# Ten of fifty dense subchunks of a graph attention's products moved from one stage to the next

## The chip, the cores and the metric

One core of one Trainium2 chip runs the whole program in one launch. The metric is the device time of that core in microseconds (us). A profile is one execution of the same program, taken by the hardware profiler.

## The reference

The program computes four residual graph layers over 100,000 nodes of 16 features and 50,000 edges sorted by destination: x = x + layer(relu(layernorm(x)), edges). The change is in the first, an attention network with two attention layers. What it computes, cut to the part that matters:

```python
def _gat_layer(x, src, dst, W, a_s, a_d, b, heads, outc):
    h = (x @ W).reshape(N, heads, outc)
    alpha_s = (h * a_s).sum(-1)
    alpha_d = (h * a_d).sum(-1)
    e = leaky_relu(alpha_s[src] + alpha_d[dst], SLOPE)
    m = segment_max(e, dst)
    p = exp(e - m[dst])
    z = segment_sum(p, dst)
    alpha = p / (z[dst] + 1e-16)
    out = segment_sum(h[src] * alpha[:, :, None], dst)
    return out.reshape(N, heads * outc) + b
# src, dst: the edges and a loop at each node
h = selu(_gat_layer(x, src, dst, W1, a_src1, a_dst1, b1, 3, 32))
h = selu(_gat_layer(h, src, dst, W2, a_src2, a_dst2, b2, 1, 32))
return h @ Wf + bf
```

A node without an incoming edge has only its own loop, so its attention is 1 and the first layer gives x @ W1 + b1 there: "dense" work that needs no edges. The others are done by "slots", one for each edge in order of destination, where the last slot of a destination holds the node's sum.

## The kernel before

The program is a row of stages, each a block in which every engine has its own list of instructions; behind each stage all engines meet at a barrier, and its semaphores are cleared. Engines wait for each other through counting semaphores (`hold`, `wait_ge`).

**Stage A** (lines 465 to 773, tiles a_...) makes three things side by side.
- DVE and PE count the edges by destination (28 groups of one-hot products for each half of the table: lines 547, 548, 652), and then DVE works out where each node's row goes.
- The dense half: 10 chunks (k) of 80 columns, each of 5 subchunks (n) of 16 columns, for all 128 partitions. SP loads a chunk of x (line 754). DVE makes its layer norm in seven pieces spread between other work (`norm_part`, lines 593 to 613, 448, 449). For a subchunk, PE transposes it (`flip`, 665), ACT copies the result to a_norm_t (715), PE makes the scores (`score`, 673), which ACT copies to a row (724), and in four quarters u: PE makes the first layer's products (`up`, 682), ACT the two activations of selu (739, 741), DVE joins them (634), PE multiplies by the second layer's weights (700), and DVE adds the constant (`send`, 624). SP stores the rows of x and scores of a chunk to t_gat1 (765) and those of the second layer of each subchunk to t_gat2 (770).
- POOL gathers the rows of x for the edges: 392 indirect DMAs (line 530), of 128 rows each. The first 112 follow the counting; the later 280 are paced by the dense half, six for the four activations of a subchunk (`joins`, a wait on act_ok). Before each batch of eight it waits until the batch before has landed.

Then comes the sorting stage (lines 778 to 960), and one that loads the sorted slots and begins to gather from t_gat1.

**Stage B** (lines 1150 to 1463, tiles g_...) is the first layer's attention over 400 slot columns. POOL gathers 336 columns of neighbours' rows (line 1208), at most about two entries ahead of DVE. DVE goes through "entries" of 48 columns (the last three of 32, 16 and 8): `edge_score` (1332 to 1345) when the entry's gathers have landed, `edge_sum` (1358 to 1372: 51 scans), `edge_mix` (1411 to 1423). Each entry feeds three chunks of 16 columns (25 in all). For a chunk: PE transposes (`flip`, 1231), ACT copies to g_mix_t (1285), PE makes four quarters of products (1245, three banks of PSUM in turn, so that the fourth waits for the first's activations), ACT two activations (1313, 1315), DVE joins (1460), PE the second products (1256), all four after one another, and DVE the rows (`send`, 1433, 1435). DVE's order by chunk: send of the chunk before, four joins, then the edge work due: the score of the next entry at the entry's second chunk, its sum and mix at the third. ACT's order: eight activations, the edge work's exponentials, and only then the copy of the next chunk.

DVE's order before, whole:

```python
for n in range(NCH):
    if n:
        send(n - 1)
    for u in range(4):
        hold(dve, exp_ok, 4 * n + u + 1)
        v.scalar_tensor_tensor(act_t[:, u], ex[:, u], 1.0, pos[:, u], ALU.min, ALU.add
                               ).then_inc(act_ok, 1)
    edges(n)
send(NCH - 1)
```

Behind stage B stands the second layer's attention, which gathers from t_gat2.

## Time and profile before

| | us |
|---|---|
| median of 3 runs | 6252.12 |
| lowest, highest | 6250.92, 6256.97 |
| the profiled execution | 6259.5 |
| its span, first to last instruction | 6257.5 |
| PE busy | 2760.5 (44%) |
| DVE busy | 3563.7 (57%) |
| ACT busy | 1272.2 (20%) |
| POOL busy | 4345.7 (69%) |
| stage A, first gather to the next stage's first DMA | 64.5 to 778.7 |
| stage B, to the next stage's first DMA | 1457.6 to 2046.4 |

PE is TensorE, DVE VectorE, ACT ScalarE, POOL GpSimd, SP the engine that only issues DMAs. Busy times overlap between engines, and none says what a stage waits for. A row of a timeline has the start in us from the span's start, the duration, the engine, the line of the kernel, the operation, and in brackets how long the engine stood idle before it and what ended that. A row of busy times by stretch has the stretch and its length, then busy us (and instructions) of PE, PEld (the weight loads), DVE, ACT and POOL, then the granted TensorE clock as a share of full speed, the DMA share and GB/s.

### The profile page before, as it was taken

To read this page: it belongs to the slowest core of one execution; us is meant where nothing else is said; L and a number is where in the kernel's file an instruction comes from. 1 tells how busy PE (TensorE), PEld (TensorE's weight loads), DVE (VectorE), ACT (ScalarE), POOL (GpSimd) and SP (SyncE) were. 2 spreads that over 40 slices of the span, in tenths; PEclk is the share of its full clock that TensorE was granted. 3 is DMA by queue.
4 is the path that set the end of the run, shared out by engine and by line. 5 is a ranking of instruction groups with operands and counts; after the bars stand their busy time and mean duration, and the time that the engine had idled before them with its cause. 6 is when DMAs were issued, how large, how long until landed. Compare 5 with 4: busy or idle time off the path is not lost. (4 is left out here: it accounts for less than half of the span.)

```text
span 6257.5 us, 46239 instructions
## 1 busy us (share of the span) xinstructions
PE 2760.5 (44%) x13424; PEld 2086.1 (33%) x13424; DVE 3563.7 (57%) x8977; ACT 1272.2 (20%) x2042; POOL 4345.7 (69%) x3949
## 2 busy tenths in 40 slices
PE   5789677753544455346655542111111035553000
PEld 2477533333434344345544432111111013432000
DVE  8855399977556666673447777433322138886000
ACT  0166377741322233211111110000000011000000
POOL 4766566667773677477767776888888844777776
PEclk9899899985665555566667675555555567776555
DMA  2022133321110422123322222222222235221001
GB/s 44 10 72 63 51 80 78 77 74 12 20 20 16 99 70 64 46 72 101 101 83 67 65 70 79 44 38 38 41 29 26 8 97 174 60 57 33 7 7 47
DMA packets 283361, 350.20 MB, mean 56 GB/s; under 512 B 133518, under 2 KB 204432, under 8 KB 281970
## 3 DMA queue, kind: packets, MB, share of 16 engines
q1 hardware_dynamic: 112158, 295.24, 14.1%
q0 software_dynamic: 169376, 41.40, 8.9%
q10 hardware_dynamic: 1576, 10.60, 0.7%
q8 instruction: 109, 1.79, 0.1%
q14 instruction: 142, 1.16, 0.1%
HBM read 231.06 MB, written 122.29 MB: 56 GB/s over the span
## 5 line engine op out<-in xcount | busy, mean ns | idle before, releaser
L2412 POOL DMA_INDIRECT acc<-l_rows,l_uniq x392 | 625.1, 1595 | 121.5 <-issue 108.6
L530 POOL DMA_INDIRECT pay<-in_x,gidx x392 | 462.4, 1180 | 239.9 <-DMA pay<-in_x,gidx 116.1
L2453 PE MATMUL ps_l<-l_msg,l_alike 128*128 128x16 f32 x784 | 176.3, 375 | 960.1 <-DVE l_msg L2516 960.1
L1547 POOL DMA_INDIRECT g_ring<-t_gat,idx x392 | 423.9, 1081 | 230.5 <-issue 112.3
L2682 POOL DMA_INDIRECT l_ring<-t_last,idx x392 | 385.1, 982 | 268.1 <-ACTq L2676 148.1
L1877 POOL DMA_INDIRECT r_ring<-t_rel,idx x392 | 427.5, 1091 | 186.4 <-issue 109.1
L2398 POOL DMA_INDIRECT l_ring<-t_mix,idx x392 | 422.4, 1078 | 155.0 <-issue 119.1
L836 POOL DMA_INDIRECT t_sort<-pay,c_pos x392 | 381.6, 973 | 207.0 <-DVE c_pos L920 103.8
L2188 POOL DMA_INDIRECT r_ring<-t_rel,idx x392 | 399.6, 1019 | 152.2 <-issue 110.7
L2453 PEld LDWEIGHTS ps_l<-l_msg,l_alike 128*128 128x128 f32 x784 | 171.0, 331 | 965.4 <-DVE l_msg L2516 965.4
L2692 POOL DMA_INDIRECT fin<-X,home_i x393 | 376.9, 959 | 119.8 <-issue 119.8
L1208 POOL DMA_INDIRECT ring<-t_gat,src_i x336 | 377.7, 1124 | 109.9 <-issue 91.4
L2723 PE MATMUL ps_l<-w_rel,l_pick 128*128 128x256 f32 x784 | 258.2, 501 | 246.1 <-DVE l_pick L2752 246.1
L2511 DVE TENSOR_SCALAR l_den<-l_ring 128x128 f32<-128x128 f32 x49 | 11.2, 229 | 560.0 <-DMA l_ring<-t_mix,idx 560.0
L2723 PEld LDWEIGHTS ps_l<-w_rel,l_pick 128*128 128x128 f32 x784 | 199.3, 261 | 304.7 <-DVE l_pick L2752 265.0
L955 PE MATMUL ps_c<-coarse,c_hit 128*128 128x400 f16 x784 | 262.1, 334 | 3.9 <-ACT c_hit L855 3.9
L955 PE MATMUL ps_c<-fine,c_hit 128*128 128x400 f16 x784 | 262.1, 334 | 0.0
L2465 ACT COPY l_rows<-ps_l 128x128 f32<-128x128 f32 x49 | 13.0, 265 | 1139.7 <-PE ps_l L2453 1139.7
L700 PE MATMUL ps_a<-w_ext,a_act_t 96*128 96x128 f32 x1600 | 224.1, 285 | 39.7 <-DVE a_row L624 39.2
L700 PEld LDWEIGHTS ps_a<-w_ext,a_act_t 96*128 96x128 f32 x1600 | 214.9, 200 | 60.4 <-DVE a_row L624 49.1
L915 DVE SCALAR_TENSOR_TENSOR c_junk<-iota_lo,lo_f,ps_c 128x400 f32<-128x400 f16 x392 | 230.9, 625 | 5.5 <-PE ps_c L955 5.5
L634 DVE SCALAR_TENSOR_TENSOR a_act_t<-a_ex,a_pos 96x512 f32<-96x512 f32 x200 | 137.3, 686 | 143.5 <-ACT a_ex L741 140.0
(540 smaller groups left out, 8470.6 us busy)
## 6 DMA issues: line engine op xcount, KB each, us to landing
c_rows_d<-row_dst SPq DMA_DIRECT2D x98, 256.0 KB
l_keys<-row_at SPq DMA_DIRECT2D x49, 512.0 KB, 4.1
l_typs<-row_typ SPq DMA_DIRECT2D x49, 512.0 KB, 3.7
g_hs<-t_gat SPq DMA_DIRECT2D x30, 660.0 KB, 4.8
acc<-r_zero SPq DMA_DIRECT2D x60, 320.0 KB
t_rel<-r_row SPq DMA_DIRECT2D x30, 640.0 KB, 3.6
r_hs<-t_rel SPq DMA_DIRECT2D x30, 640.0 KB, 4.7
d_gain<-acc SPq DMA_DIRECT2D x30, 640.0 KB
```

The costliest lines, as they stand in the source:

```text
L530: pool.indirect_dma_start(pay[:, s, 8:PAY], None, x, bass.IndirectOffsetOnAxis(gidx[:, s:s + 1], 0)).then_inc(gat_in[s // BATCH], 16)
L700: last = mm(ps[:, at:at + WIDE], act_t[:, u, P * m:P * (m + 1)], w2_ext[:], start=True, stop=True, skip_group_check=True)
L836: pool.indirect_dma_start(t_sort, bass.IndirectOffsetOnAxis(pos[:, e:e + 1], 0), pay[:, e, :], None).then_inc(sent, 16)
L955: last = mm(ps[:, bank:bank + LO], hit[:, q % 2, j, col:col + P], part[:, LO * j:LO * (j + 1)], start=(j == 0 and m == 0), stop=(j == 1 an ...
L1208: pool.indirect_dma_start(ring1[:, s, :], None, t_gat1, bass.IndirectOffsetOnAxis(src_i[:, s:s + 1], 0)).then_inc(gat_in[s // BATCH], 16)
L1547: pool.indirect_dma_start(ring[:, s % (NR * QN), :], None, t_gat2, bass.IndirectOffsetOnAxis(idx2[:, s:s + 1], 0)).then_inc(gat_in[s // BA ...
L1877: pool.indirect_dma_start(ring[:, s % (NR * QN), :], None, table, bass.IndirectOffsetOnAxis(idx2[:, s:s + 1], 0)).then_inc(gat_in[s // BAT ...
L2188: pool.indirect_dma_start(ring[:, s % (NR * QN), :], None, t_rel2, bass.IndirectOffsetOnAxis(idx2[:, s:s + 1], 0)).then_inc(gat_in[s // BA ...
L2398: pool.indirect_dma_start(ring[:, s, :], None, t_mix, bass.IndirectOffsetOnAxis(idx2[:, s:s + 1], 0)).then_inc(gat_in[s // BATCH], 16)
L2412: pool.indirect_dma_start(acc[r], bass.IndirectOffsetOnAxis(uniq[:, s:s + 1], 0), rows[:, (s // ES) % RR, s % ES, :], None, compute_op=ALU.add
L2682: pool.indirect_dma_start(ring[:, s, :], None, t_last, bass.IndirectOffsetOnAxis(idx2[:, s:s + 1], 0)).then_inc(gat_in[s // BATCH], 16)
L2723: last = mm(ps[:, at:at + 256], pick[:, e % 2, s], w_rel[:].rearrange("p i o -> p (i o)"), start=True, stop=True)
```

## The change

Every fifth dense subchunk (the last of each chunk) keeps its layer norm, transpose, copy and scores in stage A, but its products are not made there. Its transposed, normalised columns go to a tile of their own and to a new table in DRAM, t_late, of 128 x 256 numbers for each of ten. Stage B loads them two jobs ahead and works through a list of 35 jobs: dense 0 and 1, then the 25 slot chunks, with a dense job behind each odd one up to the fifteenth. POOL's pacing in stage A becomes seven gathers for four activations. In stage B the order within a job changes too: the products of the next job stand between those of this one, ACT copies the next chunk (into the other of two tiles) after the first quarter, and DVE's send comes after the first join. The diff, without renamed counters:

```diff
+    heavy = [n for n in range(NSUB) if n % PER != PER - 1]
+    NH = len(heavy)
+    assert T - 2 * NB <= 7 * NH and PER == 5 and SUB * FEAT == t_late.shape[2] and ND == t_late.shape[1]
...
+    late_s = [sem("late0"), sem("late1")]
+
+    def flat_of(n):
+        if n % PER == PER - 1:
+            return late[:, (n // PER) % 2]
+        return norm_t[:, heavy.index(n) % 3]
+
...
-        part, turn_no = divmod(s - 2 * NB, 6)
-        joins = 4 * part + (0, 1, 1, 2, 3, 3)[turn_no]
+        part, turn_no = divmod(s - 2 * NB, 7)
+        joins = 4 * part + turn_no // 2
         if part < 0 and s % 2 == 0 and s >= 4:
             hold(pool, hist_ok, s // 2 - 1)
-        elif joins > 0 and turn_no not in (2, 5):
+        elif joins > 0 and turn_no % 2 == 0:
             hold(pool, act_ok, joins)
         if s >= BATCH and s % BATCH == 0:
...
-        for n in range(NSUB):
+        for i, n in enumerate(heavy):
             if n + 2 < NSUB:
                 flip(n + 2)
             for u in range(4):
-                if n and u % 2 == 0:
-                    hold(pe, row2_ok, 2 * (n - 1) + u // 2 + 1)
-                hold(pe, act_ok, 4 * n + u + 1)
+                if u == 2 and n % PER == PER - 2:
+                    if n + 3 < NSUB:
+                        flip(n + 3)
+                    score(n + 1)
+                if i and u % 2 == 0:
+                    hold(pe, row2_ok, 2 * (i - 1) + u // 2 + 1)
+                hold(pe, act_ok, 4 * i + u + 1)
...
-                if n + 1 < NSUB:
-                    up(n + 1, u)
-            if n + 1 < NSUB:
-                score(n + 1)
+                if i + 1 < NH:
+                    up(i + 1, u)
+            if i + 1 < NH:
+                score(heavy[i + 1])
...
+            if n % PER == PER - 1:
+                if n // PER >= 2:
+                    hold(act, score_ok, n - 2 * PER + 1)
+                    act.wait_ge(late_s[(n // PER) % 2], 16 * (n // PER // 2))
+            elif heavy.index(n) >= 3:
+                hold(act, score_ok, heavy[heavy.index(n) - 3] + 1)
+            nc.scalar.copy(flat_of(n), ps[:, FLIP:FLIP + SUB * FEAT]).then_inc(copy_ok, 1)
...
+                if u == 3 and n % PER == PER - 2:
+                    if n + 3 < NSUB:
+                        turn(n + 3)
+                    take_scores(n + 1)
...
-            if n % PER == PER - 1:
-                hold(sp, scored, n + 1)
+            if n % PER == PER - 2:
+                hold(sp, scored, n + 2)
                 hold(sp, row_ok, k + 1)
                 sp.dma_start(t_gat1.rearrange("(p c) f -> p c f", c=C)[:, k * Q:(k + 1) * Q, :], row[:, k % 2]
                              ).then_inc(out_s[k % 2], 16)
                 if k + 2 < ND:
                     load(k + 2)
-            hold(sp, row2_ok, 2 * (n + 1))
-            sp.dma_start(columns_of(t_gat2, SLOTS + SUB * n, SUB), row2[:, n % 2]).then_inc(out2_s[n % 2], 16)
+                sp.dma_start(t_late[:, k], late[:, k % 2]).then_inc(late_s[k % 2], 16)
+            hold(sp, row2_ok, 2 * (i + 1))
+            sp.dma_start(columns_of(t_gat2, SLOTS + SUB * n, SUB), row2[:, i % 2]).then_inc(out2_s[i % 2], 16)
...
+    LATE = t_late.shape[1]
+    jobs = [("dense", 0), ("dense", 1)]
+    for n in range(NCH):
+        jobs.append(("slot", n))
+        if n % 2 == 1 and len(jobs) - n - 1 < LATE:
+            jobs.append(("dense", len(jobs) - n - 1))
+    NJ = len(jobs)
+    entering = [("slot", n) for n in enter]
+    job_of = [jobs.index(("slot", n)) for n in range(NCH)]
+    assert NJ == NCH + LATE
...
+    mix_t = tmp("mix_t", [HID, 2, 8 * P])
+    late_t = tmp("late_t", [P, 2, Q * FEAT])
...
+        def load(d):
+            sp.dma_start(late_t[:, d % 2], t_late[:, d]).then_inc(late_in[d % 2], 16)
+
+        load(0)
+        load(1)
+        for t, (kind, k) in enumerate(jobs):
+            at = Q * k if kind == "slot" else SLOTS + 5 * Q * k + 4 * Q
+            hold(sp, row_ok, t + 1)
+            sp.dma_start(columns_of(t_gat2, at, Q), row[:, t % 2]).then_inc(out_s[t % 2], 16)
+            if kind == "dense" and k + 2 < LATE:
+                load(k + 2)
...
+        def up(t, u):
+            kind, k = jobs[t]
+            if u == 0 and kind == "slot":
+                hold(pe, copy_ok, k + 1)
+            if u == 0 and kind == "dense":
+                hold(pe, late_in[k % 2], 16 * (k // 2 + 1))
+            if 4 * t + u >= 3:
+                hold(pe, exp_ok, 4 * t + u - 2)
+            bank = 1024 + 512 * ((4 * t + u) % 3)
+            to = ps[0:HID, bank:bank + 512]
+            for j in range(2):
+                if kind == "slot":
                     at = 512 * (u % 2) + 256 * j
                     last = mm(to[:, 256 * j:256 * (j + 1)], w1_half[:, u // 2].rearrange("p h c -> p (h c)"),
-                              mix_t[:, at:at + 256], start=True, stop=True)
-                last.then_inc(up_ok, 1)
-            if n + 1 < NCH and n + 1 not in enter:
-                flip(n + 1)
-            if n:
-                hold(pe, row_ok, n)
+                              mix_t[:, k % 2, at:at + 256], start=True, stop=True)
+                else:
+                    last = mm(to[:, 256 * j:256 * (j + 1)], w1_dense[:, 2 * u + j], late_t[:, k % 2],
+                              start=True, stop=True)
+            last.then_inc(up_ok, 1)
+
+        def down(t, u):
+            kind, k = jobs[t]
+            if t and u == 0:
+                hold(pe, row_ok, t)
+            hold(pe, act_ok, 4 * t + u + 1)
+            for m in range(4):
+                node = 2 * (4 * (u % 2) + m) + u // 2 if kind == "slot" else 8 * (m % 2) + 2 * u + m // 2
+                last = mm(ps_o[:, node // 8, node % 8], act_t[:, u, P * m:P * (m + 1)],
+                          w2_ext[:, 0:CH + 2],
+                          start=True, stop=True)
+            if u == 3:
+                last.then_inc(down_ok, 1)
+
+        for u in range(3):
+            up(0, u)
+        for t, (kind, n) in enumerate(jobs):
+            if t + 1 < NJ and jobs[t + 1][0] == "slot" and jobs[t + 1][1] not in enter:
+                flip(jobs[t + 1][1])
+            if t == 0:
+                up(0, 3)
             for u in range(4):
-                hold(pe, act_ok, 4 * n + u + 1)
-                for m in range(4):
-                    node = 2 * (4 * (u % 2) + m) + u // 2
-                    last = mm(ps_o[:, node // 8, node % 8], act_t[:, u, P * m:P * (m + 1)],
-                              w2_ext[:, 0:CH + 2],
-                              start=True, stop=True)
-            last.then_inc(down_ok, 1)
+                down(t, u)
+                if t + 1 < NJ and jobs[t + 1] not in entering:
+                    up(t + 1, u)
+            if kind == "dense":
+                if t + 1 < NJ and jobs[t + 1] in entering:
+                    flip(jobs[t + 1][1])
+                    for u in range(4):
+                        up(t + 1, u)
+                continue
...
-            if n + 1 in enter:
-                flip(n + 1)
+            if t + 1 < NJ and jobs[t + 1] in entering:
+                flip(jobs[t + 1][1])
+                for u in range(4):
+                    up(t + 1, u)
...
         def copy(n):
             hold(act, flip_ok, n + 1)
-            nc.scalar.copy(mix_t[:], ps[0:HID, 0:8 * P]).then_inc(copy_ok, 1)
+            if n >= 2:
+                hold(act, up_ok, 4 * (job_of[n - 2] + 1))
+            nc.scalar.copy(mix_t[:, n % 2], ps[0:HID, 0:8 * P]).then_inc(copy_ok, 1)
...
         edges(-1)
-        copy(0)
-        for n in range(NCH):
+        for t, (kind, n) in enumerate(jobs):
             for u in range(4):
-                hold(act, up_ok, 4 * n + u + 1)
-                bank = 1024 + 512 * ((4 * n + u) % 3)
+                hold(act, up_ok, 4 * t + u + 1)
+                bank = 1024 + 512 * ((4 * t + u) % 3)
                 view = ps[0:HID, bank:bank + 512]
                 nc.scalar.activation(pos[:, u], view, ACT.Relu, bias=b1_col[:, 1:2],
                                      scale=1.0 / SELU_ALPHA)
                 nc.scalar.activation(ex[:, u], view, ACT.Exp, bias=b1_col[:, 0:1]).then_inc(exp_ok, 1)
-            edges(n)
-            if n + 1 < NCH:
-                copy(n + 1)
+                if u == 0 and t + 1 < NJ and jobs[t + 1][0] == "slot" and jobs[t + 1] not in entering:
+                    copy(jobs[t + 1][1])
+            if kind == "slot":
+                edges(n)
+            if t + 1 < NJ and jobs[t + 1] in entering:
+                copy(jobs[t + 1][1])
...
-        def send(n):
-            b = n % 2
-            hold(dve, down_ok, n + 1)
-            if n >= 2:
-                hold(dve, out_s[b], 16 * (n // 2))
+        def send(t):
+            (kind, n), b = jobs[t], t % 2
+            hold(dve, down_ok, t + 1)
+            if t >= 2:
+                hold(dve, out_s[b], 16 * (t // 2))
             view = row[:, b].rearrange("p (a n) w -> p a n w", n=8)
-            for to, at in ((as2, CH), (ad2, CH + 1)):
+            for to, at in ((as2, CH), (ad2, CH + 1)) if kind == "slot" else ():
                 v.tensor_tensor(to[:, Q * n:Q * (n + 1)].rearrange("p (a n) w -> p a n w", n=8),
                                 ps_o[:, :, :, at:at + 1], const[:, :, :, at:at + 1], ALU.add)
...
-        for n in range(NCH):
-            if n:
-                send(n - 1)
+        for t, (kind, n) in enumerate(jobs):
             for u in range(4):
-                hold(dve, exp_ok, 4 * n + u + 1)
+                hold(dve, exp_ok, 4 * t + u + 1)
                 v.scalar_tensor_tensor(act_t[:, u], ex[:, u], 1.0, pos[:, u], ALU.min, ALU.add
                                        ).then_inc(act_ok, 1)
-            edges(n)
-        send(NCH - 1)
+                if t and u == 0:
+                    send(t - 1)
+            if kind == "slot":
+                edges(n)
+        send(NJ - 1)
```

## Rows read from the trace of the kernel before

**Rows 1.** Busy time of each engine by stretch: stage A's dense part, its end, stage B.
```profile
280.00:724.00 444.00, 403.09 (x2682) 355.47 (x2680) 246.48 (x380) 277.51 (x522) 283.94 (x250) 0.95 0.23 66
724.00:768.00 44.00, 0.00 (x0) 0.00 (x0) 0.00 (x0) 0.00 (x0) 28.44 (x31) 0.53 0.09 12
1458.00:2046.00 588.00, 276.44 (x1418) 225.25 (x1418) 367.62 (x970) 155.79 (x249) 377.67 (x336) 0.62 0.11 18
```
**Rows 2.** Timeline of stage A's end: first gathers of batches, the last, the next stage.
```profile
684.86 0.94 POOL L530 DMA_INDIRECT pay<-in_x,gidx  x1 [1.59 <-DMA pay<-in_x,gidx]
...
721.94 0.94 POOL L530 DMA_INDIRECT pay<-in_x,gidx  x1 [2.10 <-DMA pay<-in_x,gidx]
...
756.96 0.94 POOL L530 DMA_INDIRECT pay<-in_x,gidx  x1 [1.59 <-DMA pay<-in_x,gidx]
...
765.69 0.94 POOL L530 DMA_INDIRECT pay<-in_x,gidx  x1 [0.31 <-issue]
778.73 0.32 SPq L823 DMA_DIRECT2D c_rows_d<-row_dst  x1
```
**Rows 3.** Waits between 260 and 780 us: us in total, times, longest.
```profile
POOL pay L530 <- DMA pay<-in_x,gidx: 91.1, 31, 7.1
```
**Rows 4.** Waits between 1450 and 2050 us.
```profile
DVE g_act_t L1460 <- ACT g_ex L1315: 142.9, 95, 6.5
...
DVE idx L1332 <- DMA ring<-t_gat,src_i: 33.5, 6, 6.5
```
**Rows 5.** Timeline of stage A: PE's second products, two quarters on end.
```profile
699.96 1.06 PE L700 MATMUL ps_a<-w_ext,a_act_t 96*128 96x128 f32 x8
...
701.72 1.06 PE L700 MATMUL ps_a<-w_ext,a_act_t 96*128 96x128 f32 x8
```
**Rows 6.** Timeline of stage A: a gather beside DVE.
```profile
282.79 2.80 POOL L530 DMA_INDIRECT pay<-in_x,gidx  x1 [0.31 <-issue]
...
283.28 1.48 DVE L595 SCALAR_TENSOR_TENSOR a_ln_cent<-a_ln_small,a_xin 128x1280 f32<-128x1280 f32 x1
...
284.80 0.69 DVE L634 SCALAR_TENSOR_TENSOR a_act_t<-a_ex,a_pos 96x512 f32<-96x512 f32 x1
```
**Rows 7.** Timeline of stage B: one entry, from mix to mix, and cold ups.
```profile
1562.27 5.54 PE L1245 MATMUL ps_g<-g_mix_t,w_half 96*96 96x256 f32 x16 [1.10 <-ACT g_mix_t L1285]
...
1625.09 2.56 DVE L1423 TENSOR_TENSOR g_mix<-g_mix,g_S 128x2304 f32<-128x2304 f32 x1
...
1629.74 1.01 ACT L1285 COPY g_mix_t<-ps_g 96x1024 f32<-96x1024 f32 x1 [12.20 <-PE ps_g L1231]
...
1637.74 1.04 PE L1231 MATMUL ps_g<-ident,g_mix 128*96 128x128 f32 x8
...
1638.61 3.66 PE L1256 MATMUL ps_g<-w_ext,g_act_t 96*128 96x34 f32 x32
...
1642.10 3.67 PE L1245 MATMUL ps_g<-g_mix_t,w_half 96*96 96x256 f32 x16
...
1644.38 0.68 ACT L1313 ACTIVATE g_pos<-ps_g,b_col 96x512 f32<-96x512 f32 x1
...
1645.52 0.69 ACT L1313 ACTIVATE g_pos<-ps_g,b_col 96x512 f32<-96x512 f32 x1
...
1647.96 0.69 DVE L1460 SCALAR_TENSOR_TENSOR g_act_t<-g_ex,g_pos 96x512 f32<-96x512 f32 x1 [0.46 <-ACT g_ex L1315]
1655.13 0.20 DVE L1332 CAST idx<-ring 128x48 int32<-128x48 f32 x1 [6.48 <-DMA ring<-t_gat,src_i]
...
1668.03 2.54 DVE L1358 TENSOR_TENSOR g_S<-ring,ps_g 128x2304 f32<-128x2304 f32 x1
...
1694.02 2.56 DVE L1423 TENSOR_TENSOR g_mix<-g_mix,g_S 128x2304 f32<-128x2304 f32 x1
```
**Rows 8.** Timeline of stage B: the mix of entry 0 and that of entry 6.
```profile
1492.34 2.56 DVE L1423 TENSOR_TENSOR g_mix<-g_mix,g_S 128x2304 f32<-128x2304 f32 x1
...
1899.13 2.56 DVE L1423 TENSOR_TENSOR g_mix<-g_mix,g_S 128x2304 f32<-128x2304 f32 x1
```

More of the change, by code:

```diff
@@ L120, in gnn_kernel @@
     row_typ = scratch("row_typ", (T, P))
+    t_late = scratch("t_late", (P, C // 80, 256))
     w_rel_dram = scratch("w_rel_dram", (RELS * FEAT, FEAT))
@@ L499, in gnn_kernel @@
             row2 = tmp("row2", [P, 2, SUB, GAT2])
+            late = tmp("late", [P, 2, SUB * FEAT])
             t = ln_buffers(ctx, Q, "a", 2)
@@ L642, in _ @@
                     for half in range(2):
-                        send(NSUB - 1, half)
+                        send(NH - 1, half)
                 @block.tensor
@@ L690, in _ @@
                     score(0)
-                    for n in range(NSUB):
+                    for i, n in enumerate(heavy):
                         if n + 2 < NSUB:
```

59 lines of the change are left out of this document (22 added, 37 removed).

## The prediction

> **What bounds the kernel now.** I read the chip's whole span first, then the two stages that the change touches, then inside each the one engine whose waits set its end. The program runs in stages with a barrier behind each, so a stage is worth what its last engine saves. The profiled execution took 6259.5 us (its span is 6257.5), 7.4 us above the median of the runs shown, 6252.1. I make the sum against the profiled one and take off 7.4 at the end.
>
> Stage A (the dense half, lines 465 to 773) has its dense chain from 280 to 724 us, and PE is busy 403 of those 444 us. Then comes the stretch to look at: from 724 to 768 PE, DVE and ACT show zero instructions, and POOL alone runs 31 gathers [rows 1]. The stage ends with POOL: its last gather starts at 765.69, and the next stage's first DMA goes out at 778.73 [rows 2]. What holds POOL is itself: 250 gathers in 444 us are 1.78 us each, 31 in 44 us 1.42 us; its longest wait is for the landing of each batch of eight, 91.1 us in 31 waits [rows 3]. The waits on act_ok that pace it never decide: the last gather asks for activation 186 of 200, and the dense chain had made all 200 by 724.
>
> Stage B (slots of the first attention, lines 1150 to 1463, 1458 to 2046 us): PE is busy 276 of 588 us, ACT 156, DVE 368, POOL 378 [rows 1]. It looks like room for ten jobs. But DVE is a chain here. Per 48 columns (an "entry") it does sum and mix, then three chunks of activations, and in between a score that needs POOL's gathers. DVE waits 142.9 us for ACT's exponentials and only 33.5 us, in six waits, for gathers [rows 4].
>
> **Stage A, part by part.** Removed: up, activation, down and send of ten subchunks. In the steady state one quarter of up and down takes PE 1.76 us (from 699.96 to 701.72 [rows 5]), so 7.0 per subchunk and some 65 to 70 us off the dense chain. Kept for all fifty: flip, copy, score, the ten layer norms, the ten loads and ten stores of t_gat1. Of that gain the stage keeps nothing directly: the chain ended 42 us before POOL did, and now ends about 110 before. The new pacing (7 gathers per subchunk in place of 6) asks for 160 activations of 160 at the end and is met just as early. So all that counts is whether POOL gathers faster with less work beside it. Two rows of price. In the last chunk, where there are activations but no layer norm and no load, three batches go from 684.86 to 721.94: 37.08 us for 24 gathers, 1.545 each. The next three, with nothing beside them, go from 721.94 to 756.96: 35.02, 1.459 each [rows 2]. The difference, 0.086 us, times the 37 gathers that fit into 65 us at 1.78, is 3.2 us. That is my value, because activations are what is removed. Upper bound: the whole difference of 1.78 and 1.42 times 37, 13 us; that would need the layer norms and big transfers to go too, and they stay. On the other side I allow 3 us lost, since the same ten layer norms and transfers are packed into a shorter time and the ten stores of late rows (131 KB each) are new. Stage A: **-3 us** (-13 to +3).
>
> A gather does stretch beside DVE: the one at 282.79 took 2.80 us against 0.94, over a centring and the next activation [rows 6]. The Trainium skill (SBUF — State Buffer, "Who interferes with whom") has it that a tensor_tensor with two SBUF inputs takes only the read side of the port pair shared with GpSimd, and infers that descriptor generation needs the write side. By that the removed activations would give POOL nothing and stage A would gain 0; this trace speaks against the inference, since that gather ends only after two-input operations do.
>
> SP's list has ten fewer stores of t_gat2 and ten new ones of late rows; it only follows row2_ok and scored, and nobody waits for it but the buffers' next turn. ACT waits for late_s before it overwrites a late tile, two chunks (over 70 us) after the store was issued: nothing.
>
> **Stage B, part by part.** Prices [rows 7]: a chunk's ups cost PE 3.67 us, its downs 3.66, at the full clock (0.92 a quarter each), a flip 1.04; behind a long idle the ups take 5.54. Copy 1.00, two activations by ACT 1.15 per quarter, DVE's activation 0.69, its rows 1.0.
>
> An entry before, counted from the end of mix (1627.65): the copy ends 3.1 later (1630.75), the second chunk's last activation 17.9 after that (1648.65), then DVE waits until 1655.13 for gathers (6.5), scores for 2.9, reaches sum 12.9 after the score's start (1668.03), and sum and mix take 28.5 (to 1696.58). Without the wait that is 3.1 + 17.9 + 12.9 + 28.5 = 62.4; with it 68.9. So each middle entry has 6.5 us of cover, and one and a half dense jobs to put there.
>
> After, two things change. The dense jobs come in, and the order is new: ups of the next job lie between downs of this one, and ACT copies the next chunk after the first quarter. That copy waits for a flip which PE has behind the four ups. In the steady state a job followed by a slot chunk repeats: flip 1.04, copy 1.00, exponential of the second quarter 1.15, up 0.92, then three quarters of down and up 5.5, with handoffs 10 us; a job followed by a dense one 7.4.
> - Entries 2, 4, 6 (slot, dense, slot, score, slot, sum, mix): copy 3.1; ups end 5.5 and those of the dense job 12.8 after it; flip 13.9, copy 15.0, next up 17.2, its last 22.8, flip 23.8, copy 24.9, three exponentials and the activation 29.1; score 2.8; four prepared quarters of exponentials behind it 5.9; sum and mix 28.5: 69.4.
> - Entries 3 and 5 (dense, slot, slot, score, dense, slot, sum, mix): the dense job's exponentials were made during sum, so it costs DVE 3.8, but PE's downs stand ahead of the flip, and the copy ends 9.1 after mix; the next two chunks 15.6; score 2.8; dense and slot 14.4; 28.5: 70.4.
> - Entry 1 has two dense jobs ahead of the first chunk: copy 15.1 in place of 3.1, then 15.6 + 2.8 + 14.4 + 28.5: 76.4.
>
> Sum over entries 1 to 6: 76.4 + 3 x 69.4 + 2 x 70.4 = 425.4 us, against 1494.9 to 1901.7 = 406.8 before [rows 8]: +18.6. Behind it the copy's stall costs 3.5 at the chunk before the last scores, the saving and the loss of entry 7 cancel (-4, +3.7): about +22. The six gather waits, 33.5 us, are in that: they are the cover, and it is spent. What is late next is ACT's exponential, hence PE's ups.
>
> Bounds: nothing at all if every job fits (0); and 10 jobs of 7.4 less 33.5 of cover, +40, if the new order gives nothing back. Stage B: **+22 us** (0 to +40). The new load of a dense job's rows (131 KB) is issued two jobs ahead, against landings of a few us: nothing; if it were late, PE would stand. Gathers lengthen by some 4 us over the stage (40 more activations) and are off the path by 8 us.
>
> Sum: 6259.5 - 3 + 22 = 6278.5 profiled, less 7.4: **6271 us**.
>
> **Rivals.**
> - The cover is enough (28%). If PE stays at its full clock and handoffs cost less, entries come under the 68.9 of the gathers; then the stage is paced as before and only its tail grows, +3, less 3 in stage A: 6252. For: 33.5 us of waits and PE idle for over half. Against: PE idles through each sum and mix, which the jobs can't fill, and shows 0.62 as mean granted clock in stage B (0.95 in A) [rows 1], so the flip and ups behind it run at 1.2 GHz. It decides if an entry is 1 us or more shorter than I count.
> - POOL is freed (9%): the whole 13 us in stage A, with the stage B of the rival above giving 2 back: 6252 - 13 - 2 = 6237, faster. For: 0.36 us a gather of contention. Against: the last chunk's batches, above.
> - The new order gives nothing back, or PE works the whole stage at 1.2 GHz (8%): the ups then cost 5.54 in place of 3.67, 1.9 us in each of some fifteen chunks and jobs that stand on the chain, +28 on top of +22, 6299.
> - That the change doesn't do what it says: ten of fifty subchunks do move; the products are the same instructions, so there is no such case.
>
> **How the numbers follow.** 55% for my sum, 28, 9 and 8 for the rivals. About 12.5 us (0.2%) is what a measurement can tell. Slower holds most of the first case and the last: 0.60. Same holds the second and a tenth of the first's lower end: 0.30. Faster 0.10. The range leaves out the third case and the last: 6245 to 6294; the likeliest case's own is 6256 to 6290.
>
> **What would show it.** Right: no PE, DVE or ACT work in the last 100 us of stage A, POOL's last gather within a few us of 765.7; in stage B no waits of the score for gathers, entries of 69 to 71 us, ACT waiting for a flip at the copy. Wrong: a stage A shorter by over 8 us (the contention step), or scores that still wait for gathers with entries of 68.9 (the chain step).

## The result and the profile after

| | before | after |
|---|---|---|
| median, us | 6254.55 (4 runs) | 6326.93 (6319.76 to 6338.86, 4 runs) |
| ratio | | 1.0119, 95% interval 1.0103 to 1.0135 |
| the profiled execution, its span | 6259.5, 6257.5 | 6331.7, 6330.0 |
| first gather of x to the last gather's end | 64.5 to 766.6 | 64.2 to 745.7 |
| stage B, its first gather to the next stage's | 1458.3 to 2047.0 = 588.7 | 1438.3 to 2121.0 = 682.7 |

The kernel became 1.2% slower. The forecast was 6271 us with a range to 6294. Slower was right and the size was wrong: stage A gained 21 us where I had 3, and stage B lost 94 where I had 22. The stages between and behind them took the same time to within 3 us.

The busy times by stretch of the changed kernel (columns as in [rows 1]); the first two stretches answer to stage A's, the third to stage B's:

```profile
280.00:658.00 378.00, 335.15 (x2193) 294.01 (x2191) 211.05 (x319) 232.14 (x441) 247.93 (x219) 0.94 0.25 71
658.00:746.00 88.00, 0.00 (x0) 0.00 (x0) 0.34 (x1) 0.00 (x0) 57.54 (x61) 0.51 0.10 15
1438.00:2121.00 683.00, 436.98 (x1900) 366.06 (x1900) 398.21 (x1020) 201.18 (x329) 346.68 (x336) 0.59 0.12 21
1653.00:1745.00 92.00, 63.15 (x248) 54.07 (x248) 46.78 (x109) 23.09 (x37) 46.08 (x48) 0.54 0.13 23
1820.00:1895.00 75.00, 42.39 (x248) 36.50 (x248) 47.00 (x110) 22.88 (x37) 49.56 (x48) 0.70 0.15 27
```

In stage A the dense chain ends 65 us earlier (at 656), as predicted, and POOL works alone for 88 us (VectorE has one instruction of 0.34 us there). In stage B, PE is busy 437 us in place of 276: 161 us more for ten jobs. A job's ups and downs at full clock are 7.3 us [rows 7], so ten are 73, and the rest is slower instructions. The last two rows are the third and the fifth entry, which have the same 248 PE instructions each: 63 us of PE work and 92 us of time at a granted clock of 0.54, against 42 and 75 at 0.70.

The waits of stage B after:

```profile
ACT g_mix_t L1359 <- PE ps_g L1276: 194.2, 25, 15.8
DVE g_act_t L1534 <- ACT g_ex L1388: 188.1, 97, 11.5
...
DVE as L1509 <- PE ps_g L1307: 39.1, 14, 6.3
DVE g_row L1511 <- PE ps_g L1307: 30.9, 7, 6.3
...
POOL ring L1245 <- DVE g_mix L1499: 73.4, 5, 32.1
```

DVE no longer waits for gathers at all (33.5 us before, [rows 4]). The gathers now wait for the mix, and ACT's copy waits for PE's flip, 25 times (before: 101.0 us in 10 waits). The row of before that the second products' rows answer to:

```profile
DVE as L1433 <- PE ps_g L1256: 18.4, 8, 2.4
```

DVE is the chain in both kernels, and its terms give the whole loss: it is busy 30.6 us more (398.2 against 367.6), waits 45.2 more for exponentials (188.1 against 142.9) and 51.6 more for PE's second products (39.1 and 30.9 against 18.4), and 33.5 less for gathers. That is 93.9 of the 94.0 us.

Where the two entries part, in a timeline of the changed kernel. Both begin cold behind the mix and run the same instructions at the same distances, to 0.2 us, for 20 us:

```profile
1654.12 7.04 PE L1307 MATMUL ps_g<-w_ext,g_act_t 96*128 96x34 f32 x32 [8.40 <-DVE g_row L1511]
...
1660.96 1.92 PE L1276 MATMUL ps_g<-ident,g_mix 128*96 128x128 f32 x8
...
1670.63 1.04 PE L1276 MATMUL ps_g<-ident,g_mix 128*96 128x128 f32 x8
...
1671.51 0.98 PE L1307 MATMUL ps_g<-w_ext,g_act_t 96*128 96x34 f32 x8
...
1674.02 1.99 PE L1293 MATMUL ps_g<-g_mix_t,w_half 96*96 96x256 f32 x4 [1.53 <-ACT g_ex L1388]
...
1677.38 2.00 PE L1293 MATMUL ps_g<-g_mix_t,w_half 96*96 96x256 f32 x4
...
1679.17 1.76 PE L1307 MATMUL ps_g<-w_ext,g_act_t 96*128 96x34 f32 x8
...
1680.74 2.00 PE L1293 MATMUL ps_g<-g_mix_t,w_half 96*96 96x256 f32 x4
...
1838.89 0.98 PE L1307 MATMUL ps_g<-w_ext,g_act_t 96*128 96x34 f32 x8
...
1841.41 1.07 PE L1293 MATMUL ps_g<-g_mix_t,w_half 96*96 96x256 f32 x4 [1.54 <-ACT g_ex L1388]
...
1843.13 1.08 PE L1293 MATMUL ps_g<-g_mix_t,w_half 96*96 96x256 f32 x4
```

At 1671 PE is at full clock (a quarter's downs in 0.98 us) in both. After the wait for the exponential it has fallen to half in the first (a quarter's ups 1.99) and not in the second (1.07). From there a down and an up take 3.36 us (1677.38 to 1680.74) in one and 1.72 in the other, on the path, for every quarter. The granted clock beside it, the stretches of 4 us:

```profile
1669.00:1673.00 4.00, 3.49 (x21) 2.78 (x20) 0.00 (x0) 1.29 (x2) 3.04 (x4) 0.83 0.44 108
1673.00:1677.00 4.00, 2.98 (x11) 2.49 (x11) 2.07 (x3) 4.00 (x8) 2.82 (x3) 0.59 0.12 8
1677.00:1681.00 4.00, 4.00 (x16) 3.48 (x17) 0.69 (x1) 1.59 (x3) 3.08 (x4) 0.50 0.10 8
...
1840.00:1844.00 4.00, 2.59 (x16) 2.28 (x17) 1.78 (x3) 4.00 (x8) 3.09 (x4) 1.00 0.16 13
1844.00:1848.00 4.00, 3.95 (x28) 3.21 (x27) 2.18 (x6) 3.41 (x7) 3.04 (x4) 1.00 0.10 8
```

Once PE is at 1.2 GHz it can stay there although the profile shows it without any idle time:

```profile
1677.00:1697.00 20.00, 20.00 (x73) 16.88 (x73) 6.86 (x19) 5.69 (x10) 15.18 (x16) 0.50 0.14 23
```

The Trainium skill (TensorE: Matmul & The Clock Gate, Part 1) has the gate follow how busy PE has been. By that rule alone PE should have come back to 2.4 GHz here. It was busy 20 of 20 us and the granted clock was 0.50, so here the measurement decides against the rule as I read it. (Busy is counted by instructions; whether the gate counts something else, no run shows.)

### The profile page after: what moved, and what is told of

The parts are those of the page before. It is cut to its first block and busy times, and to the rows that moved or that the text cites. A ratio compares the mean times of both kernels' runs of the same rounds, so it can differ in the third digit from the quotient of the medians.

```text
span 6330.0 us, 46277 instructions
## 1 busy us (share of the span) xinstructions
PE 2852.9 (45%) x13424; PEld 2165.3 (34%) x13424; DVE 3560.3 (56%) x8967; ACT 1272.6 (20%) x2042; POOL 4307.0 (68%) x3949
## 5 line engine op out<-in xcount | busy, mean ns | idle before, releaser
L1245 POOL DMA_INDIRECT ring<-t_gat,src_i x336 | 346.7, 1032 | 182.0 <-issue 92.6
L1307 PEld LDWEIGHTS ps_g<-w_ext,g_act_t 96*128 96x128 f32 x1120 | 215.8, 280 | 48.2 <-DVE g_row L1511 25.3
L1307 PE MATMUL ps_g<-w_ext,g_act_t 96*128 96x34 f32 x1120 | 204.2, 347 | 29.5 <-DVE g_row L1511 21.7
L715 PE MATMUL ps_a<-w_ext,a_act_t 96*128 96x128 f32 x1280 | 184.4, 290 | 42.7 <-DVE a_row L635 42.1
```

Of the source, the lines that this page charges most:

```text
L1307: last = mm(ps_o[:, node // 8, node % 8], act_t[:, u, P * m:P * (m + 1)], w2_ext[:, 0:CH + 2], start=True, stop=True)
```

## The experiments

Stage A's length is given by the end of its last gather (766.6 before, 745.7 after), stage B's from its first gather to the next stage's (588.7, 682.7). How far one execution differs from another: four profiles whose stage A is that of before have 761.0 to 766.6, four with that of after 734.7 to 746.2; stage B as before took 585.8 to 588.7 in seven. Ratios are to the kernel before, run on the same chip.

### Stage A: what gives the 21 us

**a40, a20, a0** leave products of every fifth subchunk, of three in five, and of all, undone in stage A (zeros are stored in their rows, so part of the output is missing); stage B is that of before.

```diff
                         for u in range(4):
-                            hold(dve, exp_ok, 4 * n + u + 1)
+                            if n in heavy:
+                                i = heavy.index(n)
+                                hold(dve, exp_ok, 4 * i + u + 1)
```

> The kernel before with the products (up, activations, second products, send) of every fifth dense subchunk left out of stage A and its rows of t_gat2 stored as zeros; all else, stage B too, as before. So the output lacks those rows. Theory 'beside' (each subchunk of dense work beside POOL costs the gathers some 2 us): last gather at 745 us (before: 765.7), total 6254 - 21 = 6233. Theory 'fixed' (the forecast's: the contention hangs on the ten layer norms and the ten loads and stores, which stay): last gather at 762, total 6251. Stage B must stay at 588 to 589 us in both.

> The same with three of five subchunks' products left out (20 of 50 kept). 'Beside': thirty subchunks less give about 3 x 21 = 60 us, or less where the undisturbed rate of the gathers (1.46 us each) is reached: 280 gathers from 281 us give 690 as the floor, so a last gather between 690 and 706. 'Fixed': 3 x 3.2 = 10 us, 756.

> The same with all fifty subchunks' products left out and POOL's pacing on them gone; flips, copies, scores, layer norms, loads and stores all stay. It prices what is left of the contention: 'beside' has the last gather near 690 (undisturbed rate), 'fixed' near 748 (765.7 less 5 x 3.2), since layer norms and big transfers go on as before.

Measured: last gather 744.4, 726.4 and 721.8 us; ratios 0.9953 (0.9938 to 0.9967), 0.9922 (0.9906 to 0.9939), 0.9912 (0.9896 to 0.9929). So the 21 us come with the missing products, not with the change's pacing or its new stores, and the next twenty subchunks bring only 18 more, the last twenty 5. A price per gather or per activation would be a straight line; this isn't one. For a20 and a0 neither theory was right: 'beside' had 690 to 706 and 690, 'fixed' 756 and 748.

**a_split** leaves all fifty in place and moves one DMA: the load of x goes out after the second subchunk of a chunk, and no longer 0.4 us behind the 800 KB store.

```diff
-                            if k + 2 < ND:
-                                load(k + 2)
+                        if n % PER == 1 and k + 2 < ND:
+                            load(k + 2)
```

> The kernel before with SP's load of x issued at the second subchunk of a chunk in place of its last, so that the 625 KB load and the 800 KB store of t_gat1 no longer stand together. Output unchanged. If the long waits of POOL for a batch's landing (4.4 to 7.1 us, one in each chunk, some 27 us above the usual 2.1 in all) come from these two transfers standing together, they shrink by half and the last gather comes 10 to 15 us earlier, total 6240 to 6244; if they don't, nothing changes for POOL (765.7), though DVE's waits for x (57 us) go and the dense half ends some 50 us earlier.

Measured: last gather 741.4, 25 us earlier, ratio 0.9946 (0.9929 to 0.9963), with all the work still there. The kernel before shows why, once POOL's and SP's timelines are laid side by side:

```profile
546.92 0.94 POOL L530 DMA_INDIRECT pay<-in_x,gidx  x1 [0.30 <-issue]
554.33 0.94 POOL L530 DMA_INDIRECT pay<-in_x,gidx  x1 [6.46 <-DMA pay<-in_x,gidx]
...
546.59 0.38 SPq L765 DMA_DIRECT2D t_gat<-a_row  x1
547.01 0.36 SPq L754 DMA_DIRECT2D a_xin<-in_x  x1
```

The store and the load (1.4 MB) go out at 546.6 and 547.0, as the last gather of a batch does, and the drain that usually takes 1.6 to 2.2 us takes 6.46. That befell seven of the eight chunks that load x in the kernel before (gaps of 4.2 to 7.1 us), and two in the changed one (6.9 and 4.7). The dense chain gained too: its last activation is at 666.4 in place of 721.3, since x no longer comes late.

The Trainium skill (DMA: Bandwidth & Descriptors, "Issuing engines are not separate DMA queues") has it that DMAs of all issuing engines interleave on the same 16 DMA engines. The rows agree: gathers issued by POOL land late beside SP's transfers.

**after_split** is the same move in the changed kernel.

> The changed kernel with the load of x issued after the second heavy subchunk of a chunk and not behind the 800 KB store. In the kernel before, this move alone brought the last gather of stage A from 766.6 to 741.4 us; leaving 10 of 50 subchunks out brought it to 745.7. Theory that both do the same thing (they keep load and store from landing on one batch of gathers): the gains do not add, last gather 738 to 745, ratio to before 1.011 to 1.012. Theory that they are two things (landing, and less DVE work beside the gathers): they add, last gather 718 to 725, ratio 1.008 to 1.009.

Measured: last gather **764.0**, 18 us later than in the changed kernel and outside its 734.7 to 746.2, ratio 1.0156 (1.0140 to 1.0172). Neither theory foresaw a loss. POOL's waits for landing, from 280 us on, name it. The rows are of the kernel before, the changed one, a_split, after_split and a_smooth, in this order (us in total, times, longest):

```profile
POOL pay L530 <- DMA pay<-in_x,gidx: 89.0, 30, 7.1
```
```profile
POOL pay L541 <- DMA pay<-in_x,gidx: 63.7, 25, 6.9
```
```profile
POOL pay L530 <- DMA pay<-in_x,gidx: 65.8, 28, 6.2
```
```profile
POOL pay L541 <- DMA pay<-in_x,gidx: 89.9, 30, 5.8
```
```profile
POOL pay L530 <- DMA pay<-in_x,gidx: 61.7, 27, 3.8
```

The two slow stages A wait 89 and 90 us, the three quick ones 62 to 66; the 392 gathers themselves take 453 to 462 us in all five. In after_split a chunk takes 32.3 us, about two batches of gathers, and both transfers meet the end of a batch (gaps of 2.9 to 5.8 us, two in each chunk up to 540 us). So the step is one of phase: an edit to the length of a chunk moves the large transfers against the drains.

Landing isn't the whole of it, though. These rows are of before, after and a0, over all 392 gathers (busy us, mean ns, then the idle time before them and what ended it):

```profile
L530 POOL DMA_INDIRECT pay<-in_x,gidx x392 | 462.4, 1180 | 239.9 <-DMA pay<-in_x,gidx 116.1 <-issue 95.3 <-DVE a_act_t L634 18.1
```
```profile
L541 POOL DMA_INDIRECT pay<-in_x,gidx x392 | 455.5, 1162 | 226.2 <-issue 101.7 <-DMA pay<-in_x,gidx 91.2 <-DVE a_act_t L645 23.8
```
```profile
L538 POOL DMA_INDIRECT pay<-in_x,gidx x392 | 428.4, 1093 | 229.3 <-DMA pay<-in_x,gidx 115.3 <-issue 102.3 <-PE ps_a L663 11.7
```

a0 waits for landing as long as before does, and is still 45 us quicker: its gathers take 34 us less themselves, and 18 us of waits for activations are gone. The 34 us are the contention that the prediction priced; for fifty subchunks, so 6.8 for ten. Four profiles with the stage A of before (before, b_order, before_wide, order_wide) and four with that of after (after, b_plain, b_wide, plain_wide) give the shares of the change's 20 us. In the mean the gathers take 460.1 and 457.2 us, the waits for landing 107.5 and 88.6, those for activations 24.8 and 22.1, gathers and idle time together 699.0 and 678.9. So about 19 us are landing and 3 contention (profiles of one kind differ by 4 to 5 us in the gathers), 3 are waits for activations, and the pauses called issue give 5 back.

**a_smooth** is the kernel before with the load in four pieces over four subchunks, the store in two.

```diff
+                        if n % PER == PER - 1:
+                            store_part(k, 0)
+                        elif n % PER == 0 and k:
+                            store_part(k - 1, 1)
+                        if n % PER >= 1 and k + 2 < ND:
+                            load_part(k + 2, n % PER - 1)
```

> The kernel before with the same bytes in smaller pieces in stage A: the load of x (625 KB a chunk) in four pieces over four subchunks, the store of the slot rows (800 KB) in two. Landing theory (POOL waits long only where a large transfer lies over the end of a batch of gathers): the long waits of 4 to 7 us go, POOL's wait for gathers from 280 us on falls from 85 to 60 to 68 us, last gather 735 to 745 us instead of 766, ratio to before 0.994 to 0.997. Bytes theory (the same bytes take the same time from the gathers wherever they lie): last gather 758 to 768, ratio 0.999 to 1.001.

Measured: last gather 741.9, longest wait for landing 3.8 us (the last row above), ratio 0.9943 (0.9927 to 0.9960). The same bytes in smaller pieces hold the gathers less.

**a_lag** removes the full drain: a batch waits for the one before the last, as the gathers of the other stages do. **after_lag** does so in the changed kernel.

```diff
-                        if s >= BATCH and s % BATCH == 0:
-                            pool.wait_ge(gat_in[s // BATCH - 1], 16 * BATCH)
+                        if s >= 2 * BATCH and s % BATCH == 0:
+                            pool.wait_ge(gat_in[s // BATCH - 2], 16 * BATCH)
```

> The kernel before, in whose stage A a batch of eight gathers no longer waits for the batch just before it to land, but for the one before that. Landing theory: the 49 waits (135 us of gaps) go but for the pace of the activations, which now sets the end: last gather 700 to 730 us instead of 766, ratio 0.990 to 0.995. If the queue of gathers is itself full and the waits only change their name, the last gather stays at 755 to 768 and the ratio at 0.999 to 1.001.

> The same edit in the changed kernel. In it the last dense activation is at 657 us, so if the pace of the activations sets the end once the landing waits are gone, the last gather comes at 660 to 700 us instead of 746, 20 us or more before that of the kernel before with the same edit: then leaving ten subchunks out does speed the gathers up. If landing alone made the gain of 21 us, both kernels end stage A within 5 us of each other. Stage B is the changed kernel's own, with 34-column products: 665 to 685 us again.

Measured: a_lag 700.7 us, ratio 0.9928 (0.9913 to 0.9944); after_lag 676.8 us in stage A and 686.5 in stage B, ratio 0.9996 (0.9974 to 1.0018). What POOL waits for in a_lag, from 280 us on:

```profile
POOL pay L530 <- issue: 78.0, 256, 0.3
POOL pay L530 <- DVE a_act_t L634: 54.1, 23, 19.8
```

No wait for landing is left; the activations set the pace, as the theory said, and there the dense work counts: ten subchunks fewer are worth 24 us to the gathers, and 38 to the stage, which in a_lag ends with the dense chain (the next stage's first DMA is at 726.5 in a_lag and 688.8 in after_lag). But so is the load alone: with the drain removed and the load moved (lag_split_order_wide, below) the kernel with all fifty subchunks has its last gather at 680.7 and the next stage's first DMA at 692.7, 4 us behind after_lag in both. Taking the products out buys what moving one DMA buys.

### Stage B: what costs the 94 us

The change has two parts in stage B, the ten jobs and the new order. A third edit, **wide**, makes the second products with 128 columns, as stage A does, in place of 34: more work for PE, the same results used.

```diff
-                                last = mm(ps_o[:, node // 8, node % 8], act_t[:, u, P * m:P * (m + 1)],
-                                          w2_ext[:, 0:CH + 2],
-                                          start=True, stop=True)
+                                at = 3072 + 512 * (u // 2) + (CH + 2) * (4 * (u % 2) + m)
+                                last = mm(ps[:, at:at + WIDE], act_t[:, u, P * m:P * (m + 1)], w2_ext[:],
+                                          start=True, stop=True, skip_group_check=True)
```

b_order has the new order without the jobs (`LATE = 0`), b_plain the jobs in the old order:

```diff
+                    for t, (kind, n) in enumerate(jobs):
+                        for u in range(4):
+                            up(t, u)
...
+                        for u in range(4):
+                            down(t, u)
```

> The kernel before with the changed kernel's order in stage B (ups of the next chunk between the downs of this one, copy after the first quarter, send after the first join, two g_mix_t), but no dense jobs; stage A as before. Output unchanged. Stage B was 588.7 us. Theory 'order' (the new order with PE at 1.2 GHz is what costs: a chunk repeats in 13.9 us where it took 9 to 10): each of the eight or so chunk-to-chunk handovers costs 4 to 5 us, stage B 610 to 630, less the 33 us that the waits for gathers cover. Theory 'work' (the order is neutral and the ten jobs cost 9.4 us each): stage B 585 to 592.

> The changed kernel with the old order in stage B: the same 35 jobs, but a job's four ups, then the flip of the next slot chunk, then its four downs; ACT copies behind a job's eight activations; send before the joins; stage A as changed. Output unchanged. Stage B of the changed kernel is 682.7 us. 'Order': it falls to 588.7 + 10 x 8 less 33 of cover, 635 to 650. 'Work': it stays at 675 to 690.

> The changed kernel with 128 columns in place of 34 in each of stage B's second products, as stage A has them (the weights' other columns are zeros, the results are laid out in the order in which they are made, and send reads them so). Output unchanged. Theory 'clock' (with 34 columns PE stands busy and yet at 1.2 GHz, mean granted clock 0.50 to 0.67 in stage B, and a pair of a quarter's down and up takes 3.36 us; stage A's pair with 128 columns takes 1.76 at 2.4): granted clock above 0.85 in the stretches between sums, a pair at 1.8 to 2.0 us, stage B 682.7 down to 610 to 625. If the clock doesn't answer to it, the columns cost 94/2.4 GHz x 4 passes more a product or nothing, and stage B is 683 to 720.

> The kernel before with 128 columns in stage B's second products, all else as before. Output unchanged. Before, a chunk's ups and downs go at 2.4 GHz in part already, and the entries are paced by the gathers (68.4 us each). Both theories: stage B within 580 to 592 us, total within 8 us of before; it shows what wide products do without dense jobs.

> The kernel before with the new order of instructions in stage B and 128-column second products, no dense jobs: the missing corner. Stage B took 588.7 us (old order, 34 columns), 581.8 (old order, 128) and 595.8 (new order, 34). Clock theory: the new order costs only because PE then stands at 1.2 GHz more of the time; with wide products it costs 0 to 3 us: stage B 582 to 585, ratio to before 0.999 to 1.000. Order theory: the 7 us are waits that the order itself makes; stage B about 589, ratio 1.000 to 1.001, at a higher granted clock all the same.

> The changed kernel with the old order in stage B and 128-column second products. Stage B with the ten dense jobs took 682.7 us (new order, 34), 614.5 (new order, 128), 623.3 (old order, 34). Clock theory: once the products are wide the order is worth little, and what is left is the work of ten jobs: stage B 610 to 617, ratio to before 0.999 to 1.001. Order theory: the order is worth a good part of its 59 us at any clock; stage B 595 to 605, ratio 0.996 to 0.998.

Measured, stage B in us, and the ratio of the whole program:

| products | jobs | old order | new order |
|---|---|---|---|
| 34 columns | none | 588.7 (before) | 595.8 (b_order, 0.9997, 0.9987 to 1.0006) |
| 34 columns | ten | 623.3 (b_plain, 1.0012, 1.0002 to 1.0021) | 682.7 (after, 1.0119) |
| 128 columns | none | 581.8 (before_wide, 0.9991, 0.9981 to 1.0001) | 578.1 (order_wide, 0.9981, 0.9972 to 0.9991) |
| 128 columns | ten | 595.8 (plain_wide, 0.9981, 0.9970 to 0.9992) | 614.5 (b_wide, 0.9999, 0.9987 to 1.0012) |

The rows of stage B for b_order, b_plain, b_wide and plain_wide, in this order:

```profile
1453.00:2049.00 596.00, 338.13 (x1420) 284.37 (x1420) 365.47 (x970) 152.39 (x249) 372.74 (x337) 0.57 0.10 18
```
```profile
1437.00:2061.00 624.00, 370.41 (x1900) 301.86 (x1900) 400.79 (x1021) 202.60 (x329) 381.16 (x337) 0.66 0.12 23
```
```profile
1439.00:2053.00 614.00, 340.27 (x1900) 284.69 (x1900) 398.02 (x1030) 199.65 (x329) 374.17 (x336) 0.74 0.12 24
```
```profile
1426.00:2022.00 596.00, 329.40 (x1900) 273.63 (x1900) 401.39 (x1030) 200.33 (x329) 375.76 (x336) 0.74 0.12 25
```

- With 34 columns the parts don't add: order alone +7.1, jobs alone +34.6, together +94.0. Neither theory had that: b_plain lies under both ranges (635), and b_order over the work theory's 592 and under the order theory's 610, unless the 33 us of cover are taken off the latter.
- The new order slows PE only beside narrow products. At 34 columns it makes the same instructions longer, from 276 to 338 us busy without jobs (clock 0.62 to 0.57) and from 370 to 437 with them (0.66 to 0.59); at 128 columns it adds 2 us (262 in before_wide at 0.67, 264 in order_wide at 0.69) and 11 (329 and 340, both at 0.74).
- b_wide differs from the changed kernel by the columns of one product (and by where in PSUM its results lie). It gives PE more to do, and PE is busy 97 us less (340 against 437), because the granted clock goes from 0.59 to 0.74; the stage is 68 us shorter. So some 68 of the 94 us come with the clock, and 26 remain, near the 22 that I had forecast for full-clock quarters. DVE's terms give the same 26: 30 us busy more than before, 16 more for exponentials, 12 more for rows, 33.5 less for gathers. Behind three mixes of b_wide the granted clock was 0.86 up to the next score (the first stretch is 1551.8 to 1588.0 us), where the expectation asked for over 0.85.
- The order theory held in part (plain_wide is where it had it, order_wide is under both theories' ranges). At 128 columns with jobs the old order is still 19 us quicker; DVE waits 131.1 us for exponentials in plain_wide and 159.0 in b_wide. Without jobs the new one is 4 us quicker, little more than two profiles of one stage differ. ACT's longer wait for the flip is not by itself the price: it comes with the new order in both (94.6 us in 10 waits to 152.1 in 25 with jobs, 99.7 in 9 to 161.5 in 25 without).
- With 34 columns and jobs in the new order the stage is not repeatable: it took 682.7, 667.6 (after_split) and 686.5 us (after_lag), and after_lag's ten runs lie between 6229 and 6285 us. The wide stages repeat: 595.8 and 596.3 (lag_plain_wide), 578.1 and 577.3 (lag_split_order_wide). In after_split the third entry ran at 0.70 and took 75 us, where it had 92 in the changed kernel.

### What is best

> The kernel before with the two edits that made it faster alone: load of x after the second subchunk of a chunk (stage B starts at 1431.4 us instead of 1458.3) and 128-column second products in stage B (581.8 us instead of 588.7). The stages lie 690 us apart, so they should add: -27 to -30 us, ratio to before 0.993 to 0.9955. If the wide products gained nothing on their own (their interval reached 1.0001) it is 0.9946, as the load's move alone.

> No dense jobs: the kernel before with all four edits that are its own: gathers wait one batch later, load of x earlier in the chunk, new order and 128-column second products in stage B. Stage A: the activations end at 668 us with the load moved, so last gather 670 to 705 us; stage B 578 to 584 us. Sum against the kernel before: -61 to -96 in stage A and -5 to -11 in stage B, ratio 0.983 to 0.990. If the landing waits only move, stage A ends at 741 and the ratio is 0.993 to 0.995.

> The changed kernel mended as far as is known: in stage A a batch of gathers waits one batch later, in stage B the old order and 128-column second products. If the stages add: last gather 677 us as in after_lag, stage B 596 to 605 us, so 6180 to 6195 us, ratio to before 0.988 to 0.990. The kernel before with the corresponding edits and the load moved took 6156 us; if leaving ten subchunks out of stage A had a worth of its own that outweighs ten jobs in stage B, this kernel would come under 6156 us (stage B under 572 us, or the last gather under 655 us).

split_wide (before with the load moved and wide products) has 0.9946 (0.9933 to 0.9960): no more than the load alone, so the wide products' own gain in the old order wasn't to be told from nothing in the whole time (its stage B took 584.0 us, before_wide's 581.8, against 585.8 to 588.7 with narrow ones). lag_split_order_wide, no jobs and all four other edits, takes **6156.28 us (6154.48 to 6166.30), ratio 0.9835 (0.9821 to 0.9849)**: last gather 680.7, stage B 577.3. lag_plain_wide, the changed kernel mended, takes 6175.42, ratio 0.9866 (0.9850 to 0.9883): last gather 679.2, stage B 596.3. The bounds that I had set beforehand for the move to have a worth of its own (stage B under 572 us, or the last gather under 655) were not met: the jobs cost some 19 us in stage B and save nothing more in stage A than the moved load does. So the idea doesn't pay here even when both faults are gone. The changed kernel with the lag and the moved load together was not run.

## Why the prediction was wrong

- **What bounds stage A (right).** POOL set the end; the dense chain ended at 656 and nothing but POOL ran after 658.4 until the gathers were done. Two readings beside it were off: the pacing that "never decides" holds POOL for 18.1 us in 29 waits before (23.8 in 13 after), and the new pacing's last gather asks for activation 159, not 160.
- **Stage A's sum, -3 us (wrong: -21).** The step that failed is "all that counts is whether POOL gathers faster with less work beside it". I read the 91.1 us of landing waits [rows 3] as a constant, priced a gather by the activations beside it, and took the difference of 1.78 and 1.42 as the upper bound "that would need the layer norms and big transfers to go too, and they stay". They stayed, but moved against the drains: from 280 us on, 25 of the wait's 89 us went, and 5.7 came back in waits for activations. The term that I did price, contention at 3.2 us, had about the right size: the gathers themselves gave 2.9 in the mean of four profiles against four, where landing gave 19. The longest wait in that row, 7.1, against 1.6 to 2.2 for an ordinary one [rows 2], was the clue, and I had it.
- **Stage B's sum, +22 us (wrong: +94).** The terms were quarters at 0.92 us and a repeat of 10 us for a job. The changed kernel has 3.36 us for a down and an up in the slow entries, and entries of 101.8, 75.9, 92.6, 74.9, 75.1 and 74.8 where I had 76.4, 69.4, 70.4, 69.4, 70.4 and 69.4. Where most quarters ran at full clock, the same sum was nearly right: b_wide's entries take 76.7, 69.9, 73.1, 70.1, 73.2 and 70.1. What failed most was not the chain but the clock put under it. Two smaller steps were off as well. The cold ups were priced at 5.54 us, one of the shortest in stage B of before; in the entry of [rows 7] itself they took 7.10 (at 1630.80), and behind most mixes 6.6 to 7.1. And I let the new order give time back, with +40 as the bound if it gave none; at 128 columns with jobs it costs 19 us.
- **The rival that named the cause, at 8%.** "PE works the whole stage at 1.2 GHz" was the mechanism, priced at +28 on top, 6299 in all. The price took only ups at 5.54 for 3.67, on fifteen chunks. The downs go from 0.98 to 1.76 a quarter as well, the ups from 1.07 to 2.00, and in the new order both lie between one exponential and the next, so all four quarters of each job pay. I had read 0.62 as the clock behind idle stretches [rows 1], and not asked whether more work would lift it. It didn't: 0.59.
- **The wait that goes (right).** Scores no longer wait for gathers, and ACT waits for the flip at the copy.
- **Late rows, queues (right as far as seen).** The new loads cost PE's dense ups one wait of 7.3 us, for the first load as the stage begins. Those ups end at 1445.2, and DVE's first activation comes at 1474.97, right behind its mix, so that wait lay beside the path.

What stays open: why PE falls to 1.2 GHz in one entry and not in its twin after the same 20 us, and why narrow products keep it there. The runs show that the edit to the second products decides (0.59 to 0.74 in the granted clock), and that the old order raises it with narrow ones (0.59 to 0.66). That the columns do this and not the results' other places in PSUM is likely but not shown: no run took the two apart.

## What to carry to other kernels

Where an engine drains its queue of gathers, look at what else lands then: the longest wait of a row against its usual one shows it, and waiting one batch later brought the last gather from 766.6 to 700.7 us here. Price TensorE work that is put into a half-idle stage at both clocks and on every quarter of the chain, and don't count on the added work to lift the clock (ten jobs took it from 0.62 to 0.66 in the old order, and from 0.57 to 0.59 in the new one); compare the same instructions in two places of one trace. Before work is moved to another stage, see whether the engine that ends the first stage waits for that work at all.

## What the hardware showed that I had not expected

- A stage ran 68 us faster with 128 columns in its second products (1120 instructions in the trace) in place of 34, and with their results in other places of PSUM. At either clock the wider ones cost next to nothing: 32 of them cold took 7.00 us (b_wide) against 7.04, and eight at full clock 1.06 against 0.98.
- PE busy without a gap at a granted clock of 0.50 for 20 us, and the same 248 instructions at a mean of 0.54 in one entry and 0.70 in another of one execution.
- Two transfers of 1.4 MB in all, issued as a batch of small gathers ends, stretch the wait for the batch's landing from 2 to 6.5 us (7.1 at the longest); the moved load that takes this away in one kernel brings it back in the other.
